# Experts of a routed layer: two first-layer tiles of the next token group placed between a group's first and second layer

## The reference, cut to what matters

```python
logits = xt @ wg                                   # 8192 tokens, 8 experts
topv, topi = jax.lax.top_k(softmax(logits), K)     # K = 2
...
disp = disp.at[topi, pos_c].add(xk)                # (8, 2048, 256): each expert's tokens
h = jax.nn.relu(jnp.einsum('ecm,emh->ech', disp, w1) + b1[:, None, :])
y = jnp.einsum('ech,ehm->ecm', h, w2) + b2[:, None, :]
out = jnp.sum(gate[..., None] * y[topi, pos_c], axis=1)
```

## Time and profile before

| | us |
|---|---|
| median of 3 runs | 1421.14 (1421.1 to 1423.01) |
| the profiled execution, its own time | 1429.75 |
| its span, first to last instruction | 1427.9 |
| TensorE matmuls busy in the span | 1175.3 (82%) |
| VectorE | 1016.6 (71%) |
| ScalarE | 628.1 (44%) |
| GpSimd | 625.2 (44%) |

### The profile page before, as it was taken

One profiled execution on the slowest core, in us unless ns is written; L12 is line 12 of the kernel. 1 busy time (PEld: TensorE's weight loads), 2 busy tenths in 40 slices (PEclk: granted clock), 3 DMA queues, 4 the chain that ended last, 5 costly groups with the idle time before them and its releaser, 6 DMA issues. The chain is left out here.

```text
span 1427.9 us, 22572 instructions
## 1 busy us (share of the span) xinstructions
PE 1175.3 (82%) x7547; PEld 802.9 (56%) x7547; DVE 1016.6 (71%) x1931; ACT 628.1 (44%) x960; POOL 625.2 (44%) x530
## 2 busy tenths in 40 slices
PE   4899999588888884146999989999899998999910
PEld 3566666366666663134566666666666665666610
DVE  7757667759888887885767667676576765776638
ACT  4855555233333441003544545445455454553522
POOL 5500000028777777013454544645546455464430
PEclk9999999799999997557999999999999999999965
DMA  8260000001111110105555445554555545555569
GB/s 328 83 214 1 1 1 1 15 30 31 31 31 31 32 31 16 59 19 109 105 109 104 76 99 101 112 106 71 108 92 113 109 66 114 89 111 104 66 168 347
DMA packets 148960, 122.55 MB, mean 86 GB/s; under 512 B 88400, under 2 KB 133328, under 8 KB 148720
## 3 DMA queue, kind: packets, MB, share of 16 engines
q1 hardware_dynamic: 114912, 83.90, 20.1%
q0 software_dynamic: 25200, 35.85, 16.4%
q10 hardware_dynamic: 8736, 1.33, 0.5%
HBM read 58.91 MB, written 44.30 MB: 72 GB/s over the span
## 5 line engine op out<-in xcount | busy, mean ns | idle before, releaser
L1722 ACT ACTIVATE e_h_all<-e_pH,e_b1c,e_h_scale 128x512 f32<-128x512 f32 x256 | 199.6, 780 | 283.9 <-PE e_pH L1763 256.1
L1777 PE MATMUL e_pY<-e_w_hi,e_h_hi 128*128 128x256 f16 x1024 | 279.6, 273 | 17.1 <-DVE e_w_lo L1597 10.0
L1506 POOL DMA_INDIRECT e_xg<-xn_rows,e_icol x140 | 162.4, 1160 | 287.1 <-DVE e_icol L1538 254.3
L1778 PE MATMUL e_pY<-e_w_lo,e_h_hi 128*128 128x256 f16 x1024 | 279.1, 273 | 0.0
L1779 PE MATMUL e_pY<-e_w_hi,e_h_lo 128*128 128x256 f16 x1024 | 279.1, 273 | 0.0
L1521 POOL DMA_INDIRECT expert_sums<-e_yo,e_dcol x128 | 213.0, 1664 | 76.7 <-issue 43.0
L1640 DVE TENSOR_TENSOR e_h_lo<-e_h_all,e_h_hi 128x512 f16<-128x512 f32 x256 | 177.3, 693 | 66.3 <-ACT e_h_hi L1722 56.6
L1761 PE MATMUL e_pH<-e_xT,e_w_hi 128*128 128x512 f16 x512 | 195.1, 381 | 26.5 <-DMA e_xT<-e_xs 17.6
L1762 PE MATMUL e_pH<-e_xT,e_w_hi 128*128 128x512 f16 x512 | 194.9, 381 | 0.0
L1763 PE MATMUL e_pH<-e_xT,e_w_lo 128*128 128x512 f16 x512 | 194.8, 380 | 0.0
L1777 PEld LDWEIGHTS e_pY<-e_w_hi,e_h_hi 128*128 128x128 f16 x1024 | 100.1, 98 | 42.9 <-DVE e_h_lo L1640 24.6
(11 more groups left out here) (251 smaller groups left out, 2169.0 us busy)
## 6 DMA issues: line engine op xcount, KB each, us to landing
raw<-expert_w SPq DMA_DIRECT2D x18, 1024.0 KB
expert_sums<-a_zero SPq DMA_DIRECT2D x10, 1024.0 KB, 10.7
x_st<-x SPq DMA_DIRECT2D x16, 512.0 KB, 9.1
xn_rows<-c_xn SPq DMA_DIRECT2D x16, 512.0 KB, 3.0
f_ya<-expert_sums SPq DMA_DIRECT2D x16, 512.0 KB, 7.3
out<-x_st SPq DMA_DIRECT2D x8, 1024.0 KB, 8.5
e_xg<-xn_rows,e_icol POOLq DMA_INDIRECT x140
e_xT<-e_xs SPq DMA_TRANSPOSE x136
```

The costliest lines, as they stand in the source:

```text
L1506: pool.indirect_dma_start(xg[:, q, 0:D + E], None, v.xn3_dram, bass.IndirectOffsetOnAxis(icol[u][:, q:q + 1], axis=0), bounds_check=N - 1, ...
L1722: last = act.activation(dst, pH[h % NPH][:, :], ACT.Relu, bias=b1c[eu][:, h:h + 1], scale=h_scale[eu][:, 0:1])
L1777: pe.matmul(pY[:, q, :], h_hi[:, h, cols], w2_hi[:, h, :], start=(h == 0), stop=False)
L1778: pe.matmul(pY[:, q, :], h_hi[:, h, cols], w2_lo[:, h, :], start=False, stop=False)
```

## The change

TensorE's first layer becomes a function over a range of units. With EARLY = 2, groups 0 to 2 of an expert are followed, ahead of their second layer, by units 0 and 1 of the next group of the same expert; units 2 to 7 come behind it. The first group of an expert makes all its eight units in one piece. The wait for `x_turned` stands ahead of unit 0. `h_ready` now starts at 8 instead of 1, and the wait before a unit asks for the unit four before it, also across groups. ScalarE, which may now find units 0 and 1 of group n finished while the second layer of group n - 1 still reads `h_hi`, waits for `y_done` of that group before the first of them. The transposition of the maxima on TensorE and VectorE's answer to it move from unit 0 and 1 to unit 2 and 3 of group 2.

```diff
@@ -1632,7 +1633,7 @@
                     for h in range(HT):
-                        dve.wait_ge(h_ready, HT * n + h + 1 + 1)
+                        dve.wait_ge(h_ready, HT * (n + 1) + h + 1)
...
-                        if g == 2 and h == 1:
+                        if g == 2 and h == EARLY + 1:
                             largest_of_all(e + 1)
...
             @block.scalar
             def _(act):
-                act.sem_inc(h_ready, 1)
+                act.sem_inc(h_ready, HT)
...
                     for h in range(HT):
                         act.wait_ge(h_done, HT * n + h + 1)
+                        if h == 0 and g:
+                            act.wait_ge(y_done, 2 * n)
+                            act.sem_inc(passed, 1)
...
-                def body(e, eu, g, n):
+                def first_layer(e, g, n, units):
                     u = g % 2
-                    if g == 0:
-                        pe.wait_ge(w1_lo_ready, e + 1)
-                        pe.sem_inc(passed, 1)
-                    pe.wait_ge(x_turned, 16 * BLK * (n + 1))
                     x_hi, x_lo = xT[u][:, 0:KD, :], xT[u][:, KD:2 * KD, :]
-                    for h in range(HT):
-
-                        pe.wait_ge(h_ready, HT * n + max(h - NPH + 1, 0) + 1)
+                    for h in units:
+                        if h == 0:
+                            pe.wait_ge(x_turned, 16 * BLK * (n + 1))
+                        pe.wait_ge(h_ready, HT * n + h + HT - NPH + 1)
...
-                        if g == 2 and h == 0:
+                        if g == 2 and h == EARLY:
                             turn_most(e + 1)
+
+                def body(e, eu, g, n):
+
+                    if g == 0:
+                        pe.wait_ge(w1_lo_ready, e + 1)
+                        pe.sem_inc(passed, 1)
+                        first_layer(e, g, n, range(EARLY))
+                    first_layer(e, g, n, range(EARLY, HT))
+                    if g < GRPS - 1:
+                        first_layer(e, g + 1, n + 1, range(EARLY))
                     pe.wait_ge(yb_ready, 2 * n + 1)
```

More of the change, by code:

```diff
@@ L1438, in experts @@
         STEPS = 8
+        EARLY = 2
         def groups(eng, body):
```

## The result

The changed kernel took 1410.8 us (1409.83 to 1411.42, 4 runs) beside 1421.37 us (1421.1 to 1423.01, 4 runs) for the kernel before: ratio 0.9923, 95% interval 0.9905 to 0.994. That is 10.6 us less. Its profiled execution took 1410.62 us, so this time profile and timed runs agree.

What follows compares the result with a forecast made beforehand. TensorE, busy 82%, was held to lose 20.6 us waiting for last units. From 1421.14, -7.0 (short hold) gave 1414 and -10.9 (no hold) 1410, taken together as 1412 us; range 1402 to 1429, likeliest case 1409 to 1415.

Steps and rivals of the forecast that it cites:

- Group 0, -12.5 us: Group 0's second layers: two early units cover the wait for the eighth w2_lo with 0.85 us to spare, -12.5 us.
- The residual in groups 1 and 2: Waitless second layers of groups 0 to 2: the eighth unit's residual 0.1 us goes, 24 x 0.08 = -2.0 us.
- Group 3's 0.56: Group 3's second layer, with six units left before it, waits 0.56 us plus hold at the eighth h_lo, instead of 0.11.
- ScalarE's pace and start: ScalarE starts 0.35 us behind the second layer without a hold; bank 0 back at 1.9, pairs take 2.27 against TensorE's 2.59.
- hold - 0.7: TensorE's wait for PSUM bank 0 in the next group's first layer: the hold minus 0.7 us.
- What was moved past: x_turned, next expert's w1_lo, the maximum's transposition and one semaphore instruction: all stay hidden, 0 each; w1_lo with 1.2 us in hand.
- The hold: ScalarE and VectorE start late behind second layers, beyond 0.3 us: 3.2 us after group 0, 1.5 after group 2; reality doubted.
- The first sum: Short hold behind group 0, 1.5 us behind group 2: 1421.14 - 12.5 - 2.0 - 7.2 - 0.9 + 8 x (0.56 + 1.5 - 0.11) = 1414.
- What lies between two iterations: Group 3s that end between two iterations of the loop over expert pairs: taken as not touched.
- The slower rival: PSUM bank 0 in group 1: a real, staying hold halves TensorE's run ahead; 1425 or 1434 us, chance 0.29.
- gone with the new order: Behind groups 0 and 2: hold real but removed by the new order, -19 us, 1402; chance 0.10.
- It comes to nothing: Waits change place: holds of about 1.7 us behind groups 0, and those of group 3, cancel the gain; 1422, chance 0.13.

Runs made afterwards that it cites:

- the kernel before, repeated: The kernel before, nothing edited, profiled a second time: 1421.16 us.
- the artificial hold: Changed kernel with five chained activations added on ScalarE between the end of group 0's second layer and unit 0 of group 1: 1421.4 us.
- seven activations: Changed kernel with seven chained activations added on ScalarE between the end of group 0's second layer and unit 0 of group 1: 1440.22 us.

## Why the prediction was right, point by point

**Group 0, -12.5 us: right.** The eight second layers went from 96.9 us (the kernel before, repeated) to 83.8, 13.1 less, the residual 0.1 of the eighth unit among it. The cover of 0.85 us at that unit held in every expert.

**The residual in groups 1 and 2: right.** Against the repeated trace group 1 went from 84.6 to 83.85 and group 2 from 87.9 to 87.2, 1.5 for sixteen.

**Group 3's 0.56: right, slightly large.** It measured 0.49 at the eighth unit, 0.42 over the 10.57 of before, in all eight experts.

**ScalarE's pace and start: right.** Its first activation stands at 0.29 (0.35 said), bank 0 is back 1.46 later. One formula, s + 1.46 - 1.295 x (4 - k), gives the wait at the fifth unit in all four cases that had one:

| k | s | formula | trace |
|---|---|---|---|
| 3 | 0.29 | 0.46 | 0.50 |
| 2 | 2.47 | 1.34 | 1.37 |
| 2 | 3.36 | 2.23 | 2.26 |
| 1 | 2.47 | 0.05 | 0.08 |

For k = 2 and s = 0.29 it gives -0.84, and no wait is seen. The prediction's "hold - 0.7" is the same thing.

**What was moved past: right.** w1_lo of the next expert was made at 1082.04 + 2.35 = 1084.4, 1.9 us before group 3's end at 1086.31 (1.2 was said), and TensorE's first layer behind it starts without a wait. No wait for x_turned appeared ahead of the units put early.

```profile
1082.04 2.35 DVE L1591 SCALAR_TENSOR_TENSOR e_w_lo<-raw,e_scale,e_w_hi 128x2048 f16<-128x2048 f32 x1 [2.20 <-ACT e_w_hi L1690]
```

**The hold: half right.** I gave two sums, 1414 with a short hold and 1410 without one, and merged them at 1412. The reason for doubt (8.6 us between profile and median, 8.1 us of holds) was the better guide: without a hold the sum was -10.9, and -10.6 was measured. The first sum came near by luck, from terms that no timed run had. It also took 1.5 us for every hold behind group 2, and expert 0's was 3.1. The 7.2 + 0.9 us that the first sum took off were never in the timed runs. By the Trainium skill (Perfetto Trace Analysis, Tensor Engine Instruction) TensorE's notice comes with PSUM's acknowledgement; an acknowledgement that is always late is refuted as the reason, since the same program ran in the second trace without one. Whether it was the recording that held it back, as the Trainium skill (NOTIFIC — the notification-queue block, section 7.1) would allow, no run shows. It happened in one profiled execution; in all thirteen other traces, of this program and its variants, VectorE reads 0.31 to 0.33 us behind the second layers of groups 0 and 2. Its cause stays open.

**What lies between two iterations: put at nothing, which held only roughly.** Three times in the stage TensorE waits at the end of one iteration and in the first layer of the next. Over the 10.57 and 10.36 us that these layers need (10.99 and 12.95 in the changed kernel), this cost 11.6 us in the repeated trace of the kernel before and 13.0 in the changed kernel's. From trace to trace it varies by more than that: 11.6 to 14.7 in those of kernels with no unit ahead, 12.0 to 15.3 in those with some. A sum that leaves this out cannot be trusted to 0.3 us, and so the closeness of -10.9 to -10.6 is luck in part.

**The slower rival: right place and point, wrong price.** It would decide at bank 0 from a hold of 0.7 upwards; the artificial hold of 2.2 us cost 1.37 per expert there, where "hold - 0.7" gives 1.5. But for a hold of 3.07 the rule gives 2.4 x 8 = 19 us, and 29.4 came: the rival's 20 us left out that TensorE's clock can fall behind such a wait. Had the hold of 3.2 been real, its 8 x 2.5 would have been up to 8 x (2.5 + 1.7) = 34, and its 1434 nearer 1448.

**The rival "gone with the new order", 1402,** had the same false 8.1 us in it. **"It comes to nothing"** would have needed holds of 1.7 us, and there were none. The nearest to it is the run with five activations, which brings the changed kernel level with the kernel before.

## What to carry to other kernels

Before a wait of a profile is put into a sum, compare the profiled time with the median of the timed runs: an excess of the size of the waits says that they belong to that one execution, and a second profile settles it. Work put ahead of a dependent stage is paid out of the run-ahead behind it, so count both covers, the slack gained ahead (2.59 us here, 1.7 needed) and the units left until the next buffer is asked for (2.59, 1.75 needed), and take the smallest count that suffices at each place: 2, 2 and 1 units gave 1406.7 us where 2, 2 and 2 gave 1410.8. Such a change also makes the kernel more fragile: with ScalarE kept from the next group until 2.47 us behind the second layer the kernel before lost nothing (it starts at 1.5 there anyway), this one lost all it had gained, and the one with one unit ahead lost 1.1.

## What the runs showed of the hardware that I had not expected

In one execution VectorE and ScalarE saw TensorE's signal at the end of group 0's second layers 3.2 us late, in all eight experts, and in the other traced execution of the same program not at all; about 8 us hung on it.

TensorE's granted clock fell to its lower level behind a wait of 2.26 us in the middle of steady matmuls, for about 3 us, and did not behind one of 1.37. Each held in all eight experts. But the length of the wait alone does not decide it. In the run with two, two and one units ahead there was one wait of 2.0 us, between two iterations of the loop, and the clock stayed up behind it:

```profile
1001.53 0.39 PE L1763 MATMUL e_pH<-e_xT,e_w_hi 128*128 128x512 f16 x1 [1.85 <-ACT e_h_all L1727]
```

The stretch that begins with this matmul:

```profile
1001.53:1005.50 3.97, 3.97 (x19) 1.00 0.65 82
```

It stayed up even behind a wait of 3.0 us at such a place in the first trace of the kernel before (the matmul and the stretch that begins with it):

```profile
833.12 0.39 PE L1761 MATMUL e_pH<-e_xT,e_w_hi 128*128 128x512 f16 x1 [2.85 <-issue]
...
833.12:835.52 2.40, 2.40 (x12) 1.00 0.95 248
```

In the changed kernel's trace it fell 1.2 us behind a wait of 2.8 us at the same place:

```profile
828.28:831.69 3.41, 3.41 (x10) 0.50 0.77 103
```

The changed kernel with seven activations aside, the other thirteen traces have 39 such places between iterations, and the clock fell at 20 of them and nowhere else while the eight experts ran. What decides it no run here shows. So a wait that is a little longer can cost nearly twice its length: 2.26 us of waiting came to 4.0.
